# A new order of tasks and banks in the causal attention stage of a two-layer transformer block

## The chip, the core and the metric

The program runs on one core of a Trainium2 chip, in one launch. The core has five engines that work at the same time, each through its own list of instructions in order: PE (TensorE, matrix products), DVE (VectorE), ACT (ScalarE), POOL (GpSimd) and SP (SyncE, which here only issues DMAs). They wait for each other by semaphores. PE writes its results to PSUM, which has eight banks of 128 x 512 floats; the other engines read them out. The metric is the device time of one execution in microseconds (us).

## The reference

The input x is 16 sequences of 512 tokens with 128 features. The reference computes

```
x = x + layernorm( causal_attention( layernorm(x) ) )        # 16 heads of 8, 4 key/value groups, rope
x = x + layernorm( two local layers( layernorm(x) ) )        # 8 heads of 64, windows of 64, gated FFN
```

Only the first line matters here. In it q, k and v are projections of the normalised x with a bias; q and k are turned by rope; `scores = q k^T / sqrt(8)` with the later tokens masked out; `softmax` over the keys; the products with v; a last projection `out @ Wo + bo`; then a layernorm and the addition to x. Four query heads share each of the four key/value groups.

## The kernel before

The program has three stages, one after the other: `causal_attention`, `local_layers` and `last_norm`. The change is in the first.

The causal stage works through the 16 sequences in a software pipeline. The work on one sequence is cut into 198 tasks, and the table `ORDER1` lists them once, as `(part, name, argument)`, with the PSUM bank as a fourth entry where PE fills one. `walk` (line 88) goes through the table once in each step, on every engine: part 0 is done for the next sequence, part 1 for the present one, part 2 for the one before. Each engine takes only its own tasks out of the table, so the table sets the order on every engine, and nothing else does. A task that is moved from part 2 to part 1 is done one step earlier. The class `Plan` (line 24) counts from the same table how often each bank has been filled before, and `Banks` (line 116) turns these counts into waits: a PE task waits until the last content of its bank has been read (`to_fill`), a reader waits until the bank is filled (`to_read`).

The banks are `w0` and `w1` (one PSUM bank each, `a_work` in the trace) for all transposes, projections and the value products, and `pa`, `pb`, `pc` (two PSUM banks each) for the scores.

PE's tasks, with the shape of the part of the array that they use (rows x columns; the trace prints it ahead of the operand's size):

- 128x128: `x_turn`, `q_turn`, `k_turn`, `max_turn`, `attn_turn`, `u_turn` (line 615) and `o_turn` (line 700), four transposes each; `project` (626), `out_project` (711).
- 64x128: `scores` (649, with the mask added by line 654), whose only use is the row maximum; `scores_t` (673), the same products turned, for the exponentials. 22 and 24 tasks in a sequence.
- 128x32: `values` (686), 16 tasks in a sequence, one for a head of a group and a block of keys. Four of them (0 to 3, 4 to 7, ...) fill one bank.

The others: DVE does `row_max` (583, frees the bank of `scores`), `add_bias`, `high`, `divide`, `out_bias` (598), and for three layernorms `variance` (551 to 557) and `rstd`. ACT does `exp` (515, frees the bank of `scores_t`), `seed` (491 and 493, a logarithm and an exponential between `variance` and `rstd`) and copies out of the `w` banks, such as `copy_o` (519) and `copy_max` (509). POOL does `select` (472, the causal mask on the exponentials, before `values` may use them), `rope_cos`, `rope_sin`, `rope_add`, `low`, `apply` (431) and `residual`.

Within one head the chain is `scores` - `row_max` - `max_turn` - `copy_max` - `scores_t` - `exp` - `select` - `values` - `copy_o` - `o_turn` - `divide`.

The wait that a PE task makes for its bank is this:

```
which, before = self.at(name, arg, l, b)
if after and self.at(*after, l, b)[0] != which:
    self.until_read(eng, *after, l, b)
wait(eng, self.freed[which], before)
```

Of the kernel before, what the change touches and what calls it, by code (L numbers as in the profile page):

```python
# [165 lines left out]
OWN_STEPS1 = {"variance": 3, "rstd": 3, "divide": 1}  # L166

ORDER1 = [
    (0, "load", 0), (2, "select", 13), (0, "variance", 0), (2, "select", 15), (2, "scores_t", 19, "pc"),
    (2, "select", 14), (2, "exp", 23), (2, "exp", 19), (2, "values", 8, "w1"), (2, "select", 17), (2, "select", 16),  # L170
    (2, "o_turn", 1, "w0"), (2, "scores_t", 21, "pb"), (1, "row_max", 1), (0, "seed", 0), (2, "values", 9),
    (2, "divide", 1), (2, "select", 23), (2, "scores_t", 20, "pa"), (2, "select", 19), (0, "rstd", 0),
    (1, "scores", 13, "pc"), (2, "exp", 21), (2, "exp", 20), (2, "values", 10), (1, "scores", 6, "pb"),
# [5 lines left out]
    (2, "values", 15), (0, "apply", 0), (1, "row_max", 11), (1, "row_max", 16), (1, "scores", 10, "pc"),
    (0, "x_turn", 0, "w0"), (2, "copy_o", 3), (1, "scores_t", 0, "pb"), (0, "copy_x", 0), (2, "o_turn", 3, "w1"),  # L180
    (1, "exp", 0), (1, "scores", 14, "pa"), (1, "row_max", 10), (2, "divide", 3), (1, "scores_t", 3, "pc"),
    (1, "select", 0), (0, "project", 0, "w0"), (0, "project", 1, "w1"), (1, "scores_t", 1, "pb"), (1, "exp", 3),
    (1, "row_max", 14), (0, "add_bias", 0), (1, "exp", 1), (0, "add_bias", 1), (1, "scores", 5, "pa"),
    (1, "scores_t", 4, "pc"), (1, "row_max", 5), (2, "attn_turn", 0, "w1"), (1, "exp", 4), (2, "copy_attn", 0),
    (1, "max_turn", 1, "w0"), (1, "scores_t", 5, "pb"), (1, "exp", 5), (1, "select", 3), (1, "scores", 17, "pc"),
    (1, "copy_max", 1), (1, "scores_t", 2, "pa"), (0, "rope_cos", 0), (1, "select", 1), (1, "exp", 2),
    (1, "scores", 4, "pb"), (0, "rope_sin", 0), (1, "select", 5), (0, "rope_add", 0), (2, "out_project", 0, "w0"),
    (1, "row_max", 17), (1, "row_max", 4), (2, "out_bias", 0), (1, "scores_t", 7, "pa"), (1, "select", 2),
    (1, "scores", 15, "pc"), (1, "scores_t", 9, "pb"), (1, "exp", 7), (2, "load_again", 0), (1, "exp", 9),
    (1, "values", 0, "w1"), (1, "row_max", 15), (1, "scores_t", 6, "pa"), (0, "high", 0), (1, "scores_t", 8, "pc"),  # L190
    (1, "exp", 6), (1, "select", 4), (1, "values", 1), (1, "exp", 8), (1, "max_turn", 2, "w0"),
    (1, "scores", 21, "pa"), (2, "variance", 1), (0, "copy_v", 0), (1, "copy_max", 2), (1, "values", 2),
    (2, "seed", 1), (1, "values", 3), (1, "scores_t", 11, "pc"), (1, "scores_t", 14, "pb"), (1, "copy_o", 0),
    (0, "low", 0), (1, "row_max", 21), (1, "exp", 11), (1, "scores", 19, "pa"), (0, "q_turn", 0, "w1"),
    (0, "k_turn", 0, "w0"), (1, "scores_t", 10, "pc"), (1, "exp", 14), (0, "copy_q", 0), (1, "scores", 20, "pb"),
    (1, "select", 7), (0, "copy_k", 0), (2, "rstd", 1), (0, "q_turn", 1, "w1"), (2, "apply", 1), (1, "select", 6),
    (0, "k_turn", 1, "w0"), (1, "row_max", 19), (1, "scores_t", 15, "pa"), (2, "residual", 0), (1, "exp", 10),
    (1, "select", 8), (0, "copy_q", 1), (1, "scores", 18, "pc"), (2, "store", 0), (1, "row_max", 20),
    (0, "q_turn", 2, "w1"), (0, "copy_k", 1), (1, "exp", 15), (0, "q_turn", 3, "w0"), (1, "select", 9),
    (0, "copy_q", 2), (1, "select", 10), (1, "scores_t", 16, "pb"), (0, "copy_q", 3), (1, "scores_t", 17, "pa"),  # L200
    (1, "values", 4, "w1"), (1, "exp", 17), (1, "row_max", 18), (0, "scores", 8, "pc"), (1, "exp", 16),
    (2, "variance", 2), (1, "select", 11), (1, "scores_t", 12, "pa"), (2, "seed", 2), (1, "max_turn", 3, "w0"),
    (1, "values", 5), (0, "row_max", 8), (1, "copy_max", 3), (0, "scores", 12, "pb"), (1, "exp", 12),
    (1, "scores_t", 13, "pc"), (2, "rstd", 2), (1, "exp", 13), (1, "o_turn", 0, "w0"), (0, "scores", 0, "pa"),
    (0, "row_max", 12), (1, "scores_t", 18, "pb"), (0, "scores", 9, "pc"), (2, "apply", 2), (1, "values", 6),
    (1, "divide", 0), (1, "select", 12), (1, "values", 7), (2, "u_turn", 0, "w0"), (1, "exp", 18), (0, "row_max", 0),
    (1, "copy_o", 1), (0, "row_max", 9), (1, "scores_t", 23, "pb"), (0, "scores", 1, "pa"), (2, "copy_u", 0),
# [1307 lines left out]
```

## Time and profile before

| | |
|---|---|
| three runs, median (lowest to highest) | 2255.34 us (2254.31 to 2257.92) |
| the profiled execution | 2256.49 us, its span 2254.8 us |
| PE busy over the span | 2030.4 us (90%) |
| DVE, ACT, POOL busy | 1822.7 (81%), 1633.3 (72%), 1379.3 us (61%) |
| first and last PE instruction of the causal stage | at 27.5 us and 755.5 us |
| one step of the causal stage, away from its ends | 42.28 us |

The shares of the whole span mix three stages. The causal stage is a third of it, and its steps repeat: the same row of the timeline comes again 42.28 us later. So one step is enough to read. A row of the timeline gives the start, the time from the first instruction's start to the last one's end, the engine, line, operation and tiles, and how many equal instructions it merges. Matmuls overlap, so what a task takes of PE is read from its start to the start of the next task, not from its own length.

### The profile page before, as it was taken

To read this page: it belongs to the slowest core of one execution; us is meant where nothing else is said; L and a number is where in the kernel's file an instruction comes from. 1 tells how busy PE (TensorE), PEld (TensorE's weight loads), DVE (VectorE), ACT (ScalarE), POOL (GpSimd) and SP (SyncE) were. 2 spreads that over 40 slices of the span, in tenths; PEclk is the share of its full clock that TensorE was granted. 3 is DMA by queue.
4 is the path that set the end of the run, shared out by engine and by line. 5 is a ranking of instruction groups with operands and counts; after the bars stand their busy time and mean duration, and the time that the engine had idled before them with its cause. 6 is when DMAs were issued, how large, how long until landed. Compare 5 with 4: busy or idle time off the path is not lost. (4 is left out here: it accounts for less than half of the span.)

```text
span 2254.8 us, 52451 instructions
## 1 busy us (share of the span) xinstructions
PE 2030.4 (90%) x20476; PEld 1343.0 (60%) x20476; DVE 1822.7 (81%) x3455; ACT 1633.3 (72%) x3312; POOL 1379.3 (61%) x2090
## 2 busy tenths in 40 slices
PE   2999999999999369999999999899999999999971
PEld 1555555555554146666667667666766766766641
DVE  2788888888886366898998988896898899899746
ACT  1577677677677256888888888786888888888745
POOL 3588788788786574655655655564565565565403
PEclk8899999999999679999999999999999999999985
DMA  1001001001000021010010010111001001001013
GB/s 36 1 16 30 15 16 30 15 16 30 15 16 20 29 49 32 19 30 23 18 35 19 18 35 19 29 28 40 19 18 35 19 18 35 19 18 35 19 38 112
DMA packets 50547, 59.92 MB, mean 27 GB/s; under 512 B 8144, under 2 KB 43392, under 8 KB 48256
## 3 DMA queue, kind: packets, MB, share of 16 engines
q1 hardware_dynamic: 50304, 56.58, 10.1%
q8 instruction: 165, 2.70, 0.5%
q14 instruction: 78, 0.64, 0.1%
HBM read 17.90 MB, written 8.39 MB: 12 GB/s over the span
## 5 line engine op out<-in xcount | busy, mean ns | idle before, releaser
L981 POOL TENSOR_TENSOR b_part_b<-b_raw,b_tabs 128x256 f32<-128x256 f32 x512 | 432.2, 874 | 297.5 <-ACT b_raw L1040 262.9
L990 POOL TENSOR_TENSOR b_qk<-b_qk,b_part_b 128x1024 f32<-128x1024 f32 x128 | 332.0, 2594 | 270.6 <-DVE b_qk L1140 263.4
L1140 DVE TENSOR_TENSOR b_qk<-b_raw,b_tabs 128x512 f32<-128x512 f32 x256 | 298.2, 1204 | 0.1
L1241 PE MATMUL b_work<-b_w_high,b_h_high 128*128 128x512 f32 x384 | 190.4, 496 | 30.6 <-DVE b_h_low L1130 19.2
L472 POOL TENSOR_SCALAR_AFFINE_SELECT a_probs<-a_probs 128x256 f32<-128x256 f32 x512 | 205.8, 414 | 0.0
L421 POOL TENSOR_TENSOR a_idle<-a_idle 128x1 f32<-128x1 f32 x432 | 84.5, 196 | 178.8 <-ACT a_probs L515 113.9
L686 PE MATMUL a_work<-a_probs,a_v 128*32 128x512 f32 (+3 forms) x2048 | 178.1, 443 | 8.8 <-POOL a_probs L472 8.5
L1315 PEld LDWEIGHTS b_work<-b_v_even,b_pT 128*64 128x64 f32 x2048 | 137.1, 138 | 78.1 <-issue 72.5
L1061 ACT ACTIVATE b_probs<-b_sb,b_neg_max 128x128 f32<-128x128 f32 x512 | 147.9, 383 | 41.3 <-DVE b_neg_max L1162 40.9
L1067 ACT COPY b_pT<-b_work 128x512 f32<-128x512 f32 x256 | 154.3, 603 | 23.0 <-PE b_work L1305 23.0
L1029 ACT ACTIVATE b_sq<-b_work 128x1024 f32<-128x1024 f32 x128 | 131.7, 1029 | 53.3 <-PE b_work L1243 42.7
L1156 DVE TENSOR_TENSOR b_qk<-b_qk,b_rs 128x1024 f32<-128x1024 f32 x128 | 167.3, 1308 | 3.5 <-POOL b_qk L990 2.2
L583 DVE TENSOR_REDUCE a_qpack<-a_pc 128x2 f32<-128x768 f32 (+1 forms) x128 | 139.4, 1089 | 37.8 <-PE a_pc L654 37.3
L1315 PE MATMUL b_work<-b_v_even,b_pT 128*64 128x66 f32 x2048 | 168.2, 228 | 2.0 <-ACT b_pT L1067 0.8
L1315 PE MATMUL b_work<-b_v,b_pT 128*64 128x66 f32 x2048 | 168.3, 228 | 0.0
L1268 PE MATMUL b_work<-ident,b_qk 128*128 128x128 f32 x1024 | 157.2, 284 | 12.3 <-DVE b_qk L1156 9.9
L1134 DVE TENSOR_REDUCE b_ss<-b_sq 128x16 f32<-128x1024 f32 x128 | 155.1, 1212 | 15.6 <-ACT b_sq L1029 14.4
L583 DVE TENSOR_REDUCE a_qpack<-a_pa 128x2 f32<-128x1024 f32 (+3 forms) x128 | 148.0, 1156 | 15.2 <-PE a_pa L654 13.3
L1305 PE MATMUL b_work<-ident,b_probs 128*128 128x128 f32 x1024 | 155.8, 275 | 3.7 <-ACT b_kT L1048 2.0
L1268 PEld LDWEIGHTS b_work<-ident,b_qk 128*128 128x128 f32 x1024 | 123.0, 145 | 58.0 <-issue 26.0
L1305 PEld LDWEIGHTS b_work<-ident,b_probs 128*128 128x128 f32 x1024 | 123.9, 141 | 55.1 <-issue 36.0
L1242 PE MATMUL b_work<-b_w_low,b_h_high 128*128 128x512 f32 x384 | 153.9, 401 | 0.0
(211 smaller groups left out, 5528.7 us busy)
## 6 DMA issues: line engine op xcount, KB each, us to landing
b_v_even<-b_v SPq DMA_DIRECT2D x32, 528.0 KB, 4.4
b_v_even<-b_v SPq DMA_DIRECT2D x32, 396.0 KB, 5.8
a_x_in<-in_L_attn_x SPq DMA_DIRECT2D x16, 256.0 KB, 3.2
a_x_again<-in_L_attn_x SPq DMA_DIRECT2D x16, 256.0 KB, 3.5
x_scratch<-a_x SPq DMA_DIRECT2D x16, 256.0 KB, 2.4
out<-c_y SPq DMA_DIRECT2D x4, 1024.0 KB, 5.5
b_w_raw<-in_L_ffn_wqkv SPq DMA_DIRECT2D x2, 768.0 KB, 4.2
b_tabs<-tab SPq DMA_DIRECT2D x2, 512.0 KB, 4.2
```

The lines of the kernel that those rows point to most:

```text
L472: last = pool.affine_select(out=a, in_=a, compare_op=ALU.is_ge, fill=0.0, base=0, pattern=[[0, 2], [1, P]], channel_multiplier=-1)
L583: dve.tensor_reduce(qpack[:, slot, i, js[0]:js[-1] + 1, two, NEG_MAX].rearrange("p j g -> p g j"), x[:, :, 0:len(js) * w].rearrange("p g ( ...
L686: last = pe.matmul(bank_of[which][groups(g), s * P:T], v[:, slot, s, g, :], probs_of(j, fill + g % 2)[:, g // 2, col:col + T - s * P], sta ...
L981: last = pool.tensor_tensor(part_b[:, x, :].rearrange("p (h d) -> p h d", d=DH)[:, :, lo:lo + DH // 2], raw[:, i % 2, x, :].rearrange("p ( ...
L990: pool.tensor_tensor(qk[:, i], qk[:, i], part_b[:], ALU.add).then_inc(c_made, 1)
L1134: dve.tensor_reduce(ss[:, i * 16:(i + 1) * 16], sq[:].rearrange("p x (h d) -> p (x h) d", d=DH), AX, ALU.add).then_inc(ss_made, 1)
L1140: last = dve.tensor_tensor(qk[:, i, x, :].rearrange("p (h d) -> p h d", d=DH), raw[:, i % 2, x, :].rearrange("p (h d) -> p h d", d=DH), ta ...
L1156: dve.tensor_tensor(a, a, rs[:, i * 16:(i + 1) * 16].rearrange("p (h a) -> p h a", a=1).to_broadcast([P, 16, DH]), ALU.mult).then_inc(scal ...
L1241: pe.matmul(x, h_high[:, t], w_high[:, cols], start=True, stop=False)
L1268: last = pe.transpose(x[:, p * P:(p + 1) * P], qk[:, i, which, p * P:(p + 1) * P], ident[:])
L1305: last = pe.transpose(x[:, i * P:(i + 1) * P], probs[:, h % 4, i, :], ident[:])
L1315: last = pe.matmul(x[half_rows(w), i * VW:(i + 1) * VW], pT[:, h % 4, w * WIN:(w + 1) * WIN], values_, start=True, stop=True)
```

## The change

Only the table `ORDER1` changes, and with it the waits that `Plan` counts from it; they are kept in kind. The same 198 tasks stand in another order, many with another bank. In the old table PE goes through one step in 49 changes of array shape, counted round from the last entry to the first; in the new one in 41. By shape, the runs of tasks of one shape are 15 of 128x128, 12 of 128x32 and 22 of 64x128 before, and 13, 8 and 20 after. 16 tasks move from part 2 to part 1, so that they are done one step earlier (`scores_t` 19, 21 and 22, `exp` 22 and 23, `select` 13 to 17 and 23, `values` 8 and 9, `o_turn` 1, `divide` 1, and the DMA `load_again`), and two, `scores` 6 and `row_max` 1, from part 1 to part 0. Since the table is one line longer, every line number below it is one higher.

```
-    (0, "load", 0), (2, "select", 13), (0, "variance", 0), (2, "select", 15), (2, "scores_t", 19, "pc"),
+    (0, "load", 0), (0, "variance", 0), (2, "select", 18), (2, "exp", 21), (2, "exp", 19), (1, "row_max", 6),
...
-    (2, "select", 21), (2, "divide", 2), (2, "select", 22), (1, "row_max", 7), (2, "values", 13),
-    (1, "scores", 11, "pb"), (1, "scores", 16, "pa"), (1, "max_turn", 0, "w0"), (2, "values", 14), (1, "copy_max", 0),
+    (1, "row_max", 7), (2, "values", 12, "w0"), (2, "values", 13), (2, "values", 14), (2, "values", 15),
+    (1, "scores", 11, "pb"), (2, "copy_o", 3), (1, "max_turn", 0, "w1"), (0, "x_turn", 0, "w0"), (1, "row_max", 13),
```

PE around `values` 12 to 15 of the sequence before, in a step of the old program: two of them (L686), `scores` 11 and 16 (L649 and L654), `max_turn` 0 (L615), then the other two.

```order
L686 MATMUL a_work<-a_probs,a_v 32x512 x4
L686 MATMUL a_work<-a_probs,a_v 32x384 x4
L649 MATMUL a_pb<-a_kT,a_qT 128x384 x2
L654 MATMUL a_pb<-a_mask_half,a_half_of 128x128 x2
L654 MATMUL a_pb<-a_mask_half,a_half_of 128x64 x2
L649 MATMUL a_pa<-a_kT,a_qT 128x512 x2
L654 MATMUL a_pa<-a_mask_half,a_half_of 128x128 x2
L654 MATMUL a_pa<-a_mask_half,a_half_of 128x64 x2
L615 MATMUL a_work<-ident,a_qpack 128x128 x4
L686 MATMUL a_work<-a_probs,a_v 32x256 x4
L686 MATMUL a_work<-a_probs,a_v 32x128 x4
```

The same place in the new program, from `o_turn` 2 on: `scores` 13 into `pc`, `values` 12 to 15, `scores` 11, `max_turn` 0 and `x_turn`.

```order
L701 MATMUL a_work<-ident,a_oT 128x128 x4
L650 MATMUL a_pc<-a_kT,a_qT 128x512 x2
L655 MATMUL a_pc<-a_mask_half,a_half_of 128x128 x2
L655 MATMUL a_pc<-a_mask_half,a_half_of 128x64 x2
L687 MATMUL a_work<-a_probs,a_v 32x512 x4
L687 MATMUL a_work<-a_probs,a_v 32x384 x4
L687 MATMUL a_work<-a_probs,a_v 32x256 x4
L687 MATMUL a_work<-a_probs,a_v 32x128 x4
L650 MATMUL a_pb<-a_kT,a_qT 128x384 x2
L655 MATMUL a_pb<-a_mask_half,a_half_of 128x128 x2
L655 MATMUL a_pb<-a_mask_half,a_half_of 128x64 x2
L616 MATMUL a_work<-ident,a_qpack 128x128 x4
```

The four value tasks of a head, two visits to the 128x32 shape before, are one visit now.

PE later in the step, before: `values` 1 (L686), `max_turn` 2, `scores` 21 into `pa`, `values` 2 and 3, `scores_t` 11 and 14 (L673), `scores` 19 into `pa` again.

```order
L686 MATMUL a_work<-a_probs,a_v 32x384 x4
L615 MATMUL a_work<-ident,a_qpack 128x128 x4
L649 MATMUL a_pa<-a_kT,a_qT 128x512 x2
L654 MATMUL a_pa<-a_mask_half,a_half_of 128x128 x2
L654 MATMUL a_pa<-a_mask_half,a_half_of 128x64 x2
L686 MATMUL a_work<-a_probs,a_v 32x256 x4
L686 MATMUL a_work<-a_probs,a_v 32x128 x4
L673 MATMUL a_pc<-a_qmT,a_kT 128x256 x2
L673 MATMUL a_pb<-a_qmT,a_kT 128x384 x2
L673 MATMUL a_pb<-a_qmT,a_kT 128x128 x2
L649 MATMUL a_pa<-a_kT,a_qT 128x384 x2
```

The same stretch after: `scores_t` 7 and 6 (the latter into `pb`), `max_turn` 2, `values` 1 to 3, `scores` 20 into `pa`, `scores_t` 11, `q_turn` 0 and `k_turn` 1, and `scores` 21 into `pb`.

```order
L674 MATMUL a_pc<-a_qmT,a_kT 128x512 x2
L674 MATMUL a_pb<-a_qmT,a_kT 128x512 x2
L616 MATMUL a_work<-ident,a_qpack 128x128 x4
L687 MATMUL a_work<-a_probs,a_v 32x384 x4
L687 MATMUL a_work<-a_probs,a_v 32x256 x4
L687 MATMUL a_work<-a_probs,a_v 32x128 x4
L650 MATMUL a_pa<-a_kT,a_qT 128x512 x2
L655 MATMUL a_pa<-a_mask_half,a_half_of 128x128 x2
L655 MATMUL a_pa<-a_mask_half,a_half_of 128x64 x2
L674 MATMUL a_pc<-a_qmT,a_kT 128x256 x2
L616 MATMUL a_work<-ident,a_qpack 128x128 x4
L616 MATMUL a_work<-ident,a_kpack 128x128 x4
```

`max_turn` 2 now stands between `values` 0 and `values` 1, and the second fill of one bank close behind another, `scores` 21 and 19 in `pa`, is gone; instead `scores` 21 fills `pb` behind `scores_t` 6.

ACT in the same stretch of the new program: `exp` 9, 8 and 7, `copy_max` 2 (L510), `seed` 1 (L492 and L494), `copy_o` 0 (L520), `exp` 6 out of `pb`, and the first copies of q and k.

```order
L516 ACTIVATE a_probs<-a_pc 128x1024
L516 ACTIVATE a_probs<-a_pa 128x1024
L516 ACTIVATE a_probs<-a_pc 128x1024
L510 CAST a_qmT<-a_work 128x512
L492 ACTIVATE a_seed<-a_var 128x4
L494 ACTIVATE a_seed<-a_seed 128x4
L520 COPY a_oT<-a_work 128x512
L516 ACTIVATE a_probs<-a_pb 128x1024
L506 CAST a_qT<-a_work 128x512
L502 CAST a_kT<-a_work 128x512
```

Before, all of head 1's first exponentials (`exp` 6 to 9) stood ahead of `seed` 1; now `exp` 6 stands behind it, and with it the bank `pb`.

## Rows read from the trace of the kernel before

**Rows 1.** Stretches: us, busy us (instructions) PE, PEld, DVE, ACT, POOL, clock, DMA.

```profile
318.65:360.93 42.28, 40.96 (x433) 24.72 (x429) 36.41 (x78) 30.71 (x49) 34.65 (x84) 1.00 0.08 21
706.00:758.00 52.00, 28.15 (x253) 14.13 (x251) 17.15 (x72) 23.24 (x38) 29.50 (x74) 0.78 0.06 16
```

**Rows 2.** PE's waits in that step: waited for, us in total, times, longest.

```profile
PE a_pa L649 <- DVE a_qpack L583: 0.7, 1, 0.7
PE a_work L686 <- POOL a_probs L472: 0.4, 1, 0.4
```

**Rows 3.** PE's timeline: start, us, engine, line, operation, tiles, count, idle before.

```profile
318.65 0.66 PE L615 MATMUL a_work<-ident,a_xn 128*128 128x128 f32 x4
319.23 0.50 PE L673 MATMUL a_pb<-a_qmT,a_kT 64*128 64x512 f32 x2
319.66 0.66 PE L700 MATMUL a_work<-ident,a_oT 128*128 128x128 f32 x4
...
322.53 0.50 PE L673 MATMUL a_pb<-a_qmT,a_kT 64*128 64x512 f32 x2
322.87 0.39 PE L649 MATMUL a_pa<-a_kT,a_qT 64*128 64x256 f32 x4
...
323.25 0.36 PE L673 MATMUL a_pc<-a_qmT,a_kT 64*128 64x256 f32 x2
...
338.44 1.09 PE L615 MATMUL a_work<-ident,a_qpack 128*128 128x128 f32 x8
339.46 0.39 PE L673 MATMUL a_pb<-a_qmT,a_kT 64*128 64x256 f32 x2
...
345.39 0.48 PE L673 MATMUL a_pb<-a_qmT,a_kT 64*128 64x512 f32 x2
345.70 0.40 PE L649 MATMUL a_pc<-a_kT,a_qT 64*128 64x512 f32 x2
...
348.94 1.07 PE L686 MATMUL a_work<-a_probs,a_v 128*32 128x512 f32 x8
349.94 0.66 PE L700 MATMUL a_work<-ident,a_oT 128*128 128x128 f32 x4
...
350.96 0.85 PE L686 MATMUL a_work<-a_probs,a_v 128*32 128x384 f32 x8
351.74 0.50 PE L673 MATMUL a_pa<-a_qmT,a_kT 64*128 64x384 f32 x4
...
353.96 0.50 PE L649 MATMUL a_pa<-a_kT,a_qT 64*128 64x256 f32 x4
354.30 0.34 PE L654 MATMUL a_pa<-a_mask_half,a_half_of 64*128 64x256 bf16 x4
354.45 0.36 PE L673 MATMUL a_pc<-a_qmT,a_kT 64*128 64x256 f32 x2
354.89 0.50 PE L649 MATMUL a_pb<-a_kT,a_qT 64*128 64x256 f32 x4
355.23 0.34 PE L654 MATMUL a_pb<-a_mask_half,a_half_of 64*128 64x256 bf16 x4
...
356.56 1.71 PE L686 MATMUL a_work<-a_probs,a_v 128*32 128x512 f32 x16
358.20 0.44 PE L649 MATMUL a_pb<-a_kT,a_qT 64*128 64x384 f32 x2
...
360.93 0.66 PE L615 MATMUL a_work<-ident,a_xn 128*128 128x128 f32 x4
```

**Rows 4.** DVE's timeline in the same step: `high`, and a `row_max` of 1024 columns.

```profile
329.49 0.75 DVE L571 CAST a_qpack<-a_turned 128x512 fp32r<-128x512 f32 x1 [0.35 <-POOL a_turned L447]
...
333.24 1.23 DVE L583 TENSOR_REDUCE a_qpack<-a_pa 128x2 f32<-128x1024 f32 x1
```

**Rows 5.** ACT's timeline behind it: the end of `seed` 1, and an `exp`.

```profile
333.47 0.20 ACT L493 ACTIVATE a_seed<-a_seed 128x4 f32<-128x4 f32 x1
...
334.54 1.03 ACT L515 ACTIVATE a_probs<-a_pb 128x1024 f32<-128x1024 f32 x1
```

More of the change, by code:

```diff
@@ L168 @@
 ORDER1 = [
-    (0, "load", 0), (2, "select", 13), (0, "variance", 0), (2, "select", 15), (2, "scores_t", 19, "pc"),
[L170 to L173, printed above, removed]
@@ L174 @@
-    (2, "values", 11), (1, "row_max", 13), (1, "scores", 3, "pa"), (1, "row_max", 6), (2, "select", 18),
-    (1, "row_max", 3), (2, "scores_t", 22, "pc"), (2, "copy_o", 2), (1, "scores", 2, "pb"), (2, "exp", 22),
-    (1, "row_max", 2), (2, "select", 20), (2, "o_turn", 2, "w0"), (1, "scores", 7, "pc"), (2, "values", 12, "w1"),
-    (2, "select", 21), (2, "divide", 2), (2, "select", 22), (1, "row_max", 7), (2, "values", 13),
-    (1, "scores", 11, "pb"), (1, "scores", 16, "pa"), (1, "max_turn", 0, "w0"), (2, "values", 14), (1, "copy_max", 0),
@@ L179 @@
[L179 to L207, printed above, removed]
+    (0, "load", 0), (0, "variance", 0), (2, "select", 18), (2, "exp", 21), (2, "exp", 19), (1, "row_max", 6),
@@ new lines @@
+    (0, "seed", 0), (2, "select", 21), (2, "scores_t", 20, "pb"), (2, "values", 10), (2, "values", 11),
+    (1, "scores", 2, "pc"), (2, "exp", 20), (1, "scores", 3, "pa"), (0, "rstd", 0), (2, "copy_o", 2),
+    (2, "select", 19), (1, "scores", 7, "pb"), (2, "o_turn", 2, "w1"), (2, "select", 20), (1, "row_max", 2),
+    (2, "select", 22), (2, "divide", 2), (1, "scores", 13, "pc"), (0, "apply", 0), (1, "row_max", 3),
+    (1, "row_max", 7), (2, "values", 12, "w0"), (2, "values", 13), (2, "values", 14), (2, "values", 15),
@@ new lines @@
+    (1, "scores", 11, "pb"), (2, "copy_o", 3), (1, "max_turn", 0, "w1"), (0, "x_turn", 0, "w0"), (1, "row_max", 13),
+    (1, "row_max", 11), (1, "scores", 16, "pa"), (1, "copy_max", 0), (1, "scores_t", 0, "pc"),
+    (1, "scores_t", 3, "pb"), (0, "copy_x", 0), (1, "row_max", 16), (0, "project", 0, "w1"), (1, "scores", 10, "pa"),
+    (0, "add_bias", 0), (1, "exp", 0), (1, "scores_t", 1, "pc"), (1, "exp", 3), (1, "row_max", 10),
+    (0, "project", 1, "w0"), (2, "o_turn", 3, "w1"), (1, "select", 0), (1, "scores_t", 4, "pa"), (0, "add_bias", 1),
@@ new lines @@
+    (2, "divide", 3), (1, "scores", 14, "pb"), (1, "exp", 1), (1, "exp", 4), (1, "row_max", 14),
+    (1, "scores", 5, "pc"), (1, "select", 3), (1, "select", 1), (0, "rope_cos", 0), (1, "row_max", 5),
+    (2, "attn_turn", 0, "w1"), (2, "copy_attn", 0), (1, "scores_t", 5, "pa"), (1, "exp", 5), (1, "scores", 4, "pb"),
+    (1, "max_turn", 1, "w0"), (1, "scores", 17, "pc"), (1, "scores_t", 2, "pa"), (1, "copy_max", 1),
+    (2, "out_project", 0, "w1"), (0, "rope_sin", 0), (1, "row_max", 4), (1, "row_max", 17), (1, "exp", 2),
@@ new lines @@
+    (1, "scores", 15, "pb"), (2, "out_bias", 0), (0, "copy_v", 0), (1, "select", 4), (1, "scores_t", 9, "pc"),
+    (1, "scores_t", 8, "pa"), (0, "rope_add", 0), (1, "exp", 9), (1, "row_max", 15), (1, "values", 0, "w1"),
+    (1, "scores_t", 7, "pc"), (1, "select", 5), (1, "scores_t", 6, "pb"), (1, "max_turn", 2, "w0"), (1, "exp", 8),
+    (1, "exp", 7), (0, "high", 0), (1, "select", 2), (1, "copy_max", 2), (1, "values", 1), (2, "variance", 1),
+    (1, "values", 2), (2, "seed", 1), (1, "values", 3), (1, "copy_o", 0), (1, "scores", 20, "pa"), (2, "rstd", 1),
@@ new lines @@
+    (1, "scores_t", 11, "pc"), (1, "row_max", 20), (0, "low", 0), (0, "q_turn", 0, "w0"), (0, "k_turn", 1, "w1"),
+    (1, "exp", 6), (1, "scores", 21, "pb"), (0, "copy_q", 0), (2, "apply", 1), (1, "scores_t", 10, "pa"),
+    (0, "copy_k", 1), (1, "exp", 11), (0, "q_turn", 2, "w0"), (0, "k_turn", 0, "w1"), (1, "scores", 18, "pc"),
+    (1, "row_max", 21), (1, "scores_t", 14, "pb"), (1, "exp", 10), (1, "select", 6), (0, "copy_q", 2),
+    (0, "copy_k", 0), (1, "scores", 19, "pa"), (1, "row_max", 18), (2, "residual", 0), (0, "q_turn", 1, "w0"),
@@ new lines @@
+    (0, "q_turn", 3, "w1"), (1, "select", 11), (1, "exp", 14), (1, "scores_t", 15, "pb"), (0, "copy_q", 1),
+    (1, "row_max", 19), (0, "copy_q", 3), (1, "select", 7), (1, "o_turn", 0, "w0"), (1, "max_turn", 3, "w1"),
+    (1, "select", 8), (1, "scores_t", 16, "pc"), (2, "variance", 2), (1, "select", 10), (1, "exp", 15),
+    (1, "copy_max", 3), (0, "scores", 12, "pa"), (1, "exp", 16), (1, "select", 9), (1, "scores_t", 17, "pb"),
+    (1, "exp", 17), (1, "values", 4, "w1"), (1, "scores_t", 18, "pc"), (2, "seed", 2), (1, "load_again", 0),
@@ new lines @@
+    (2, "store", 0), (1, "exp", 18), (1, "scores_t", 13, "pb"), (0, "row_max", 12), (0, "scores", 9, "pa"),
+    (1, "values", 5), (2, "rstd", 2), (0, "row_max", 9), (1, "values", 6), (1, "exp", 13), (0, "scores", 8, "pc"),
+    (1, "scores_t", 12, "pa"), (1, "exp", 12), (1, "divide", 0), (0, "scores", 0, "pb"), (0, "row_max", 8),
+    (1, "select", 17), (1, "values", 7), (2, "apply", 2), (0, "scores", 1, "pc"), (1, "scores_t", 23, "pa"),
+    (2, "u_turn", 0, "w0"), (1, "copy_o", 1), (0, "row_max", 0), (0, "row_max", 1), (1, "o_turn", 1, "w1"),
@@ L208 @@
+    (1, "select", 15), (1, "exp", 23), (1, "scores_t", 21, "pb"), (1, "scores_t", 22, "pa"), (1, "select", 12),
+    (1, "divide", 1), (1, "select", 13), (1, "select", 14), (1, "select", 16), (1, "scores_t", 19, "pc"),
+    (1, "values", 8, "w1"), (1, "values", 9), (1, "select", 23), (2, "copy_u", 0), (1, "exp", 22),
+    (0, "scores", 6, "pa"),
 ]
```

## The prediction

> **What bounds the kernel now.** I read the shares of the page first, then the stretches, then PE's waits, then PE's timeline. The page only says that PE is busiest, over three stages that have nothing to do with each other. The stretch of one step of the causal stage says more: from one `x_turn` to the next are 42.28 us, and PE is busy for 40.96 of them, DVE for 36.41, POOL for 34.65 and ACT for 30.71, at the full granted clock [rows 1, 3]. So PE sets the step, with 1.32 us idle. The waits name where most of that is: 0.7 us before a `scores` for the bank `pa`, which DVE's `row_max` frees late, and 0.4 us before a `values` for POOL's `select` [rows 2]. That leaves two things that a new order can change: what PE's own work takes, and these waits. PE's work is the same list of matmuls. But the same task does not take the same time everywhere.
>
> **What a change of array shape costs.** The time of a task is read from its start to the next one's [rows 3].
> - Four transposes alone between tasks of the 64x128 shape: 319.23 - 318.65 = 0.58. Eight in one run: 339.46 - 338.44 = 1.02. Two runs made one save 2 x 0.58 - 1.02 = 0.14.
> - `values` of 512 columns alone: 349.94 - 348.94 = 1.00; of 384 columns: 351.74 - 350.96 = 0.78; the two in one run: 358.20 - 356.56 = 1.64. Again 0.14 for a run less.
> - `scores_t` of 512 columns inside a run: 345.70 - 345.39 = 0.31; first in a run: 322.87 - 322.53 = 0.34; alone: 319.66 - 319.23 = 0.43. So entering costs 0.03 and leaving 0.09.
> - `scores` of 2 x 256 columns inside a run: 323.25 - 322.87 = 0.38; first in a run: 354.45 - 353.96 = 0.49. Entering costs 0.11.
> - The same `scores` behind a wait inside a run (it starts at 354.89) takes as long to its mask as the one that enters: 0.34 in both. A wait inside a run costs the entrance once more, 0.11.
>
> **The change, part by part.** 128x128 has 2 runs less: -0.28 us in a step. 128x32 has 4 less, `values` 12 to 15 in one visit among them: -0.56. 64x128 has 2 less, but what its runs begin with changes: 10 of 22 began with `scores`, 13 of 20 do now. Before: 22 x 0.09 + 10 x 0.11 + 12 x 0.03 = 3.44; after: 20 x 0.09 + 13 x 0.11 + 7 x 0.03 = 3.44. Nothing. If leaving costs 0.05 or 0.13 instead, this comes to -0.2 or +0.1. PE's work: -0.84 us in a step (-1.0 to -0.7).
>
> The waits. The 0.7 us went to `scores` 19, which refilled `pa` close behind `scores` 21. In the new order `pa` goes from `scores` 20 to `scores_t` 10, and to `scores` 19 only five PE tasks after that: gone. The 0.4 us went to `values` 1. Now `max_turn` 2 stands ahead of it, 0.58 of work that covers it; POOL has one `select` and the copy of v more to do before the `select` in question, so between 0 and 0.7 may be left. I take 0, since the move on PE alone is larger than the wait.
>
> New waits, both at places where a bank is refilled:
> - `scores` 13 takes `pc` from `scores` 2, so it waits for `row_max` 2. PE has `scores` 2 (0.49), `scores` 3 and 7 (about 0.38 each, one leaving) and `o_turn` 2 (0.58) in between, 1.8 in all. `scores` 2 lands about 0.68 after its start (from 353.96 to the end of the mask at 354.30 + 0.34), and a `row_max` takes 1.2 [rows 3, 4]: 1.9, and 0.1 for two semaphores. So at least 0.2; ahead of `row_max` 2 stand `row_max` 6 and the three steps of `rstd` 0, and I take 0.4.
> - `scores` 21 takes `pb` from `scores_t` 6, and so waits for `exp` 6, which stands on ACT behind `copy_o` 0 and `seed` 1; and `seed` 1 waits for DVE's `high` and `variance` 1. From the start of `high` to the end of `seed` 1 the trace of before has 329.49 to 333.67, 4.2 us without a gap [rows 4, 5]. `high` can start about 1.6 after `scores` 15 does (`out_bias` and `row_max` 15 are ahead). Then `copy_o` 0 (about 0.5) and `exp` 6 (1.03): 7.3. PE's work from `scores` 15 to `scores` 21 is about 6.6, estimated by kind from rows 3: two `scores` 0.8, five `scores_t` 1.8, four `values` 2.4, three sets of transposes 1.6. Some 0.6 is left as idle time, in `scores` 21 itself or in the `q_turn` ahead of it, which waits for POOL's `low` behind the same `high`.
> - Small ones, `scores_t` 10 behind `row_max` 20 among them: 0.2, as before (1.32 less 0.7 and 0.4).
>
> New sum of waits 1.2, against 1.3: -0.1. All of them stand where the shape changes anyway, while three of the old ones (`scores` 19, 2 and 4) stood inside a run and cost the entrance again, 3 x 0.11: -0.3. Bounds: all waits gone, -1.6; `values` 1 kept at 0.7 and `scores` 13 at twice its size, +0.7.
>
> A step: -0.84 - 0.1 - 0.3 = -1.24, 42.28 to about 41.0. With 16 sequences there are 14 steps in which all three parts run: -17.4. The first and last steps: PE is idle for nearly half of the end [rows 1], so saved work counts for little; the moved tasks leave the end emptier, but the chain through the last layernorms stays. I take -1, between -3 and +2. The two later stages are untouched. Together -18.4: the profiled execution's 2256.49 would be 2238.1. The median of the runs is 1.15 below that execution, so 2255.34 - 18.4 = 2236.9, and I say 2237. With the ends above, a step saves between 0.3 (work -1.0 to -0.7, waits up to +0.4 net of the restarts) and 2.0: 2247 to 2227. SP has nothing new to wait for: `load_again` is issued a step earlier, for a buffer that was read in the step before.
>
> One rule speaks on just this. The Trainium skill, page "TensorEngine Tiling (Array Packing)", section "Key Properties", says that changing the tiling mode, not merely the tile, drains TensorE. The trace agrees that it costs (0.14 for a run of transposes). As a drain it would be the same for every change; the trace has 0.03 for entering with `scores_t` and 0.11 with `scores`. What a uniform price would give is the first rival.
>
> **The rivals.**
> - *Every change costs the same.* The whole cost before is 15 x 0.14 + 12 x 0.14 + 3.44 = 7.22 us a step, 0.147 for each of 49. Eight less: -1.18; with waits and restarts -1.58, x 14 and the ends: -23.1, 2232. For it: the entrance of `scores` may be a matter of which weights come next and not of the shape. Against: three pairs of rows that show otherwise. The drain rule would be borne out by this.
> - *The work saved turns into waiting.* DVE is busy for 36.41 of 42.28, and a loop through DVE, ACT and PE (`scores`, `row_max`, `max_turn`, `exp`, `values`) might hold the step where it is: the 1.24 come back at `scores` 13 and 21. Then only the ends move: 2254. For: new waits stand behind DVE and ACT. Against: even at 41.0 DVE has 4.6 us to spare, and the longest old wait on it goes.
> - *Slower.* `seed` 1 holds up ACT, and with it `copy_o` 0, `exp` 6 and the bank `pb`. Each us by which `out_project`, `out_bias` or `high` comes later than I count goes one to one into `scores` 21. From 1.84 us there instead of 0.6 nothing is gained; at 2.8 a step is 1.0 longer, 14 x 1.0 = 14, 2269. For it: `exp` 6 stood ahead of `seed` 1 before. Against: the path was counted with an unbroken row of the trace, and `out_project` and `out_bias` have no new wait that I can find.
> - *The change doesn't do what it says*: the count of 49 and 41 is of the table and certain; nothing here.
>
> **How the numbers follow.** Forecast 0.74, uniform price 0.10, work into waiting 0.09, slower 0.07. Within 0.2% (4.5 us, about what a measurement can tell from no change) lies only the third case. Faster 0.84, same 0.09, slower 0.07. The forecast's own range, 2227 to 2247, holds the first rival too, and leaves out about 0.16; it stays as it is.
>
> **What would show it.** A step of about 41.0 between two `x_turn`; `values` 12 to 15 in about 2.4 with one entrance; no wait of `values` 1 and of `scores` 19; waits of some 0.4 at `scores` 13 behind `row_max` and 0.6 around `q_turn` 0 and `scores` 21 behind ACT; PE's busy time in a step down by about 1 us, to 39.8 or so. I am wrong if PE's busy time falls by less than 0.5, if its waits in a step exceed 2, or if a step still takes 42.

## The result and the profile after

| | before | after |
|---|---|---|
| four runs each, median (lowest to highest) | 2256.6 us (2254.31 to 2257.92) | 2220.18 us (2218.19 to 2221.09) |
| the profiled execution, its span | 2256.49, 2254.8 us | 2221.09, 2219.4 us |
| one step of the causal stage | 42.28 us | 39.73 us |

The ratio is 0.9838, with an interval of 0.9821 to 0.9856. The forecast was faster, 2237, with a range of 2227 to 2247: the sign is right, but the time lies 7 us below the range, and the gain is twice as large, 36 us instead of 18.

Nearly the whole gain lies in the steps. In the trace of before, the third of the 16 `x_turn` stands at 107.19 us and the last at 656.93: 13 steps in 549.74. After, it is 105.99 to 622.98, 516.99: 32.75 less, 2.52 a step. The two steps ahead of these give 1.8, the part behind the last `x_turn` 2.2 (98.6 to 96.4 until PE's last instruction of the stage); the first `x_turn` comes 0.6 later, and the later stages take 0.7 more.

The stretch of one step after, and of the stage's end (to 2.5 us past PE's last instruction, as in [rows 1]): us, then busy us (instructions) of PE, PEld, DVE, ACT, POOL, clock, DMA.

```profile
344.60:384.33 39.73, 39.53 (x431) 25.03 (x430) 35.61 (x79) 30.01 (x48) 34.68 (x84) 1.00 0.08 21
669.90:721.90 52.00, 28.84 (x268) 16.18 (x262) 17.72 (x73) 24.57 (x40) 29.14 (x73) 0.79 0.04 11
```

PE is idle for 0.20 us of a step, against 1.32 in [rows 1], and its busy time is down by 1.43. The view of PE's waits for this stretch, which had two rows before [rows 2], has none. PE's timeline of the places that the prediction spoke of: start, us, engine, line, operation, tiles, count.

```profile
359.11 0.36 PE L674 MATMUL a_pc<-a_qmT,a_kT 64*128 64x256 f32 x2
359.62 0.66 PE L616 MATMUL a_work<-ident,a_qpack 128*128 128x128 f32 x4
360.11 0.60 PE L616 MATMUL a_work<-ident,a_kpack 128*128 128x128 f32 x4
360.64 0.50 PE L650 MATMUL a_pb<-a_kT,a_qT 64*128 64x512 f32 x2
...
378.36 0.50 PE L650 MATMUL a_pc<-a_kT,a_qT 64*128 64x256 f32 x4
378.71 0.34 PE L655 MATMUL a_pc<-a_mask_half,a_half_of 64*128 64x256 bf16 x4
378.86 0.48 PE L650 MATMUL a_pa<-a_kT,a_qT 64*128 64x256 f32 x4
379.18 0.34 PE L655 MATMUL a_pa<-a_mask_half,a_half_of 64*128 64x256 bf16 x4
379.33 0.42 PE L650 MATMUL a_pb<-a_kT,a_qT 64*128 64x384 f32 x2
379.59 0.26 PE L655 MATMUL a_pb<-a_mask_half,a_half_of 64*128 64x128 bf16 x4
379.78 0.66 PE L701 MATMUL a_work<-ident,a_oT 128*128 128x128 f32 x4
380.44 0.49 PE L650 MATMUL a_pc<-a_kT,a_qT 64*128 64x512 f32 x2
380.77 0.26 PE L655 MATMUL a_pc<-a_mask_half,a_half_of 64*128 64x128 bf16 x4
380.96 2.36 PE L687 MATMUL a_work<-a_probs,a_v 128*32 128x512 f32 x32
383.25 0.44 PE L650 MATMUL a_pb<-a_kT,a_qT 64*128 64x384 f32 x2
```

`values` 12 to 15 take one visit of 383.25 - 380.96 = 2.29. `scores` 13 starts 0.66 after `o_turn` 2, where a set of transposes takes 0.58 [rows 3]: it waits 0.08, not 0.4. `q_turn` 0 starts 0.51 after a `scores_t` of 256 columns that leaves its run, where this takes 0.29 (323.25 to the next task at 323.54 in the trace of before): 0.22 of waiting. `scores` 21, at 360.64, starts 0.53 after `k_turn` 1, which is what transposes inside a run take before they leave: it does not wait.

What DVE and ACT did there, after: `high` and the last operation of `variance` 1; the end of `seed` 1, `copy_o` 0 and `exp` 6; and `row_max` 2.

```profile
355.51 0.48 DVE L572 CAST a_qpack<-a_turned 128x512 fp32r<-128x512 f32 x1
357.69 0.99 DVE L558 TENSOR_SCALAR a_var<-a_mv 128x4 f32<-128x4 f32 x1
379.16 1.23 DVE L584 TENSOR_REDUCE a_qpack<-a_pc 128x4 f32<-128x1024 f32 x1 [0.29 <-PE a_pc L655]
```

```profile
358.95 0.21 ACT L494 ACTIVATE a_seed<-a_seed 128x4 f32<-128x4 f32 x1
359.06 0.57 ACT L520 COPY a_oT<-a_work 128x512 f32<-128x512 f32 x1
359.52 1.03 ACT L516 ACTIVATE a_probs<-a_pb 128x1024 f32<-128x1024 f32 x1
```

From the start of `high` to the end of `seed` 1 are 359.16 - 355.51 = 3.65, not the 4.2 of [rows 4, 5]. `exp` 6 ends at 360.55, and `scores` 21 follows at 360.64. `row_max` 2 had nothing ahead of it: DVE was idle for 0.29 before.

### Where the gain came from

A wait on PE is larger than the idle time that a row shows, because the end of a matmul in the trace lies behind the point from which the next one could start. Two waits of a step before, beside the same kind of task without one: a `scores_t` of 384 columns inside a run, and the `scores` behind it.

```profile
325.12 0.48 PE L673 MATMUL a_pa<-a_qmT,a_kT 64*128 64x384 f32 x4
325.65 0.50 PE L649 MATMUL a_pb<-a_kT,a_qT 64*128 64x256 f32 x4
...
333.46 0.40 PE L673 MATMUL a_pb<-a_qmT,a_kT 64*128 64x384 f32 x4
334.52 0.44 PE L649 MATMUL a_pa<-a_kT,a_qT 64*128 64x384 f32 x2 [0.65 <-DVE a_qpack L583]
...
337.68 0.50 PE L673 MATMUL a_pa<-a_qmT,a_kT 64*128 64x384 f32 x4
338.02 0.39 PE L649 MATMUL a_pc<-a_kT,a_qT 64*128 64x384 f32 x2
```

Without a wait this takes 0.34 with the entrance, so 0.31 inside a run. `scores` 19 comes 1.06 after: 0.75 of waiting, where its row says 0.65. `scores` 4 comes 0.53 after: 0.22 of waiting, and its row says nothing, since 325.12 + 0.48 reaches to 0.05 before it.

I measured every PE task of a step in this way, against the usual time of its kind and place from start to start.

| us in a step | before | after |
|---|---|---|
| PE's work by kind and place, without waits | 39.99 | 39.19 |
| the rest of the step: waits and restarts | 2.28 | 0.55 |
| of it at places that can be named | 2.2: `scores` 19 0.74, `values` 1 0.43, `scores` 2 0.24, `scores` 4 0.21, `u_turn` 0.14, `o_turn` 2 0.13, `out_project` 0.13, `q_turn` 0 0.10, `max_turn` 0 0.08 | 0.86: `q_turn` 0 0.22, `scores_t` 10 0.22, `attn_turn` 0.11, `scores` 7, `o_turn` 2, `values` 7 and `scores` 13 0.07 to 0.08 each |

Not every entry is a wait. `o_turn` 2, `out_project` and `q_turn` 0 of before (0.36) stand behind `scores` 2, 4 and 19, which had waited themselves: these are the entrances paid again that the prediction had at 0.33. `attn_turn`, `scores` 7 and `o_turn` 2 of after (0.26), and `max_turn` 0 of before (0.08), stand behind a `scores` that itself follows another `scores`, and there the second one takes some 0.09 more without a wait (last section). The three of after can't be waits: the `divide`, `exp` and `copy_o` that they need ended at 349.79, 378.85 and 379.32, and they start at 350.09, 379.33 and 379.78. Without these entries the lists come to 2.1 before, 0.36 of it restarts, and 0.6 after. So the table can be wrong by some 0.2: waits and restarts fell by 1.5 to 1.7, and the work by 0.8 to 1.0. Some two thirds of the gain are waits.

### The profile page after: what moved, and what is told of

It reads as the page before. It is cut to its first block and busy times, and to the rows that moved or that the text cites. A ratio compares the mean times of both kernels' runs of the same rounds, so it can differ in the third digit from the quotient of the medians.

```text
span 2219.4 us, 52419 instructions
## 1 busy us (share of the span) xinstructions
PE 2010.5 (91%) x20476; PEld 1350.0 (61%) x20476; DVE 1806.2 (81%) x3455; ACT 1623.4 (73%) x3312; POOL 1380.4 (62%) x2090
## 5 line engine op out<-in xcount | busy, mean ns | idle before, releaser
L584 DVE TENSOR_REDUCE a_qpack<-a_pa 128x2 f32<-128x1024 f32 (+2 forms) x128 | 143.7, 1122 | 44.0 <-PE a_pa L655 41.4
L687 PE MATMUL a_work<-a_probs,a_v 128*32 128x512 f32 (+3 forms) x2048 | 164.9, 440 | 0.2
L1244 PE MATMUL b_work<-b_w_high,b_h_low 128*128 128x512 f32 x384 | 154.1, 401 | 0.0
```

Source lines behind the costliest of these rows:

```text
L687: last = pe.matmul(bank_of[which][groups(g), s * P:T], v[:, slot, s, g, :], probs_of(j, fill + g % 2)[:, g // 2, col:col + T - s * P], sta ...
```

## The experiments

Each ratio is to runs of before on the same chip. Kernels whose name begins with old have the old order, and those with new the new one.

**old_s19 and old_var: is the longest old wait a gap of its own?** `scores` 19 waits 0.74 us in each of 14 steps. Two ways to remove it alone, in the old order: the task moves two PE places, or the operation of DVE that delays it changes its form.

```
-    (1, "scores", 19, "pa"), (0, "q_turn", 0, "w1"), (0, "k_turn", 0, "w0"),
+    (0, "q_turn", 0, "w1"), (0, "k_turn", 0, "w0"), (1, "scores", 19, "pa"),
```

> The old order with one task moved: `scores` 19, the one that waits 0.7 us for `pa`, stands behind `k_turn` 0 instead of ahead of `q_turn` 0; still 49 changes of shape. If the wait is a local one (the bank comes free late and nothing else hangs on it), it goes, with the repeated entrance: a step of 42.28 - 0.8 = 41.5, some 12 us less in all. If the old step was held by a chain through DVE and ACT that comes round once a step (`out_project`, `variance` 1, `seed` 1, `apply` 1, `residual`, `variance` 2, `apply` 2, `u_turn`), PE only waits elsewhere: at `q_turn` 0 for `w1` and at `u_turn`, about 0.5 each, and the step stays at 42.3 (2255 to 2257 us).

```
-                step(dve.tensor_scalar(var_3[:, k], mv[:, :, 1], EPS, None, ALU.add))
+                step(dve.scalar_tensor_tensor(var_3[:, k], mv[:, :, 1], EPS, mv[:, :, 1], ALU.add, ALU.max))
```

> The old order, unchanged, with the last instruction of `variance` as a scalar_tensor_tensor (x + eps, then the maximum with x: the same value). In the trace of before this instruction, on four numbers, takes 1.31 us in `variance` 1 and ends when POOL's copy in `low` ends (333.20 against 333.17); I expect about 0.25 us of the new form, as for the other scalar_tensor_tensor of that size. If a chain through it holds the old step: 42.28 - 0.9 = 41.4, about 14 us less, with the wait of `scores` 19 nearly gone and 49 changes of shape as ever. If only changes of shape matter: nothing, 2256 us. If the instruction takes as long in the new form (POOL holds DVE up whatever it runs): nothing too, and its row says so.

old_s19: 2257.33 us, ratio 1.0004 (0.9994 to 1.0013), a step of 42.33: nothing. PE's waits in a step of old_s19 (waited for, us in total, times, longest):

```profile
PE a_work L686 <- POOL a_probs L472: 0.5, 1, 0.5
PE a_work L615 <- POOL a_z L431: 0.4, 1, 0.4
PE a_work L615 <- ACT a_oT L519: 0.4, 1, 0.4
```

The row of `scores` 19 [rows 2] is gone, and two new ones stand there: `u_turn` behind `apply` 2 (0.14 before, 0.48 from start to start now), and `q_turn` 0 behind `copy_o` 0 (about 0.4). old_var: 2252.49, ratio 0.9987 (0.9978 to 0.9997), 2.7 us. Its operation took 1.04 instead of 1.31 (0.25 was expected), the wait of `scores` 19 fell from 0.74 to 0.14, and that of `u_turn` rose to 0.49. So this wait is no gap that can be closed by itself: what is saved at one place is waited for at the next, behind POOL or ACT.

**old_u and old_s19_u: are these the two ends of one chain?** If the old step is held from `out_project` through the layernorm's steps to `u_turn`, then `u_turn` moved later, together with `scores` 19, sets it free.

```
-    (2, "u_turn", 0, "w0"), (1, "exp", 18),
...
-    (0, "scores", 1, "pa"), (2, "copy_u", 0),
+    (0, "scores", 1, "pa"), (2, "u_turn", 0, "w0"), (2, "copy_u", 0),
```

> Old order, with `u_turn` moved six table entries later, behind the next PE tasks (50 changes of shape instead of 49). In the old order `u_turn` waits 0.145 us a step for `apply` 2, while `scores` 19 waits 0.74 us. If the old step is held by the chain from `out_project` through the three layernorm steps to `u_turn`, then the place of `scores` 19 still holds it first and this alone gives at most the 0.145, less an entrance of about 0.11: step 42.2 to 42.4, 2254 to 2258. If each wait counted for itself, the same 0.145 would go: not told apart here. It is the control for the next kernel.

> Old order, with both moves: `scores` 19 behind `k_turn` 0, and `u_turn` six entries later. `scores` 19 alone gave nothing (step 42.31), since the wait turned up at `u_turn` (0.145 to 0.48). Chain theory: the two waits are the two ends of one chain, so with both loosened the 0.48 at `u_turn` goes, less one more entrance (0.11): step 41.9 to 42.0, 2250 to 2252, though neither move alone gives anything. Rival (there is a further wait that takes it, `scores_t` 23 or `scores` 2 for `pb`): 42.2 or more, 2255. From the waits that remain (`q_turn` 0 about 0.37, `values` 1 about 0.5) even the chain theory leaves the old order far above the new one.

old_u: 2257.6, ratio 1.0005 (0.9996 to 1.0015), a step of 42.46, above the expected 42.2 to 42.4: the wait of `u_turn` went, but `scores` 1, behind which PE now changes shape, takes 0.17 more, and `values` 1 waits 0.09 longer in most steps. old_s19_u: 2254.56, ratio 0.9996 (0.9986 to 1.0006), 42.17. One step of old_s19_u, as stretch and as PE's waits:

```profile
360.27:402.44 42.17, 41.04 (x433) 24.72 (x429) 36.63 (x78) 30.23 (x49) 34.67 (x84) 1.00 0.07 20
```

```profile
PE a_work L686 <- POOL a_probs L472: 0.5, 1, 0.5
PE a_work L615 <- ACT a_oT L519: 0.4, 1, 0.4
```

The 0.4 at `u_turn` is gone, and a step is 0.16 shorter than in old_s19, where 0.3 to 0.4 was expected. Some 0.15 went to one more change of shape, 0.13 to `scores` 2 and `scores_t` 23, which wait longer for `pb`, and 0.07 to `values` 1. So the chain explains where the wait of `scores` 19 went, but it is not the one thing that holds the old step: `values` 1 behind POOL and `q_turn` 0 behind ACT stay, with 0.9 together. My theory of a single chain falls. What is shown is that two moves on PE don't bring the old order's waits below about 2.0 a step; the new one has 0.55. Which of its other moves does that (of PE's tasks, of banks, or on the other engines) was not taken apart.

**new_split: how much is the shape, how much the waits?** In the new order four `scores` move between tasks of another shape, so that 49 changes stand there again, as before, and the waits stay.

```
-    (2, "values", 10), (2, "values", 11), (1, "scores", 2, "pc"),
+    (2, "values", 10), (1, "scores", 2, "pc"), (2, "values", 11),
...
+    (1, "max_turn", 0, "w1"), (1, "scores", 16, "pa"), (0, "x_turn", 0, "w0"),
...
-    (1, "row_max", 11), (1, "scores", 16, "pa"), (1, "copy_max", 0),
...
+    (1, "values", 5), (0, "scores", 8, "pc"), (2, "rstd", 2),
...
-    (1, "exp", 13), (0, "scores", 8, "pc"), (1, "scores_t", 12, "pa"),
...
+    (1, "values", 8, "w1"), (0, "scores", 6, "pa"), (1, "values", 9),
...
-    (1, "exp", 22), (0, "scores", 6, "pa"),
```

> The new order with four tasks moved so that the 41 changes of shape are 49 again: `scores` 8 between `values` 5 and 6, `scores` 6 between `values` 8 and 9, `scores` 2 between `values` 10 and 11, `scores` 16 between `max_turn` 0 and `x_turn`. By the rows: 4 runs more of 128x32 or 128x128 at 0.14, 4 more of 64x128 at 0.09 for leaving, entrances 3 x 0.03 + 0.11: 1.1 us a step, 40.8, about 16 us over the changed kernel, 2236. By a uniform price of 0.147: 1.2, 2237. If the gain was in the waits alone: 39.7 and 2220. If the new order had only moved waits about: new ones here, and more than 2240.

2236.57 us, ratio 0.9912 (0.9896 to 0.9929). The stretch of one step, and two places of it:

```profile
352.71:393.52 40.81, 40.60 (x433) 24.84 (x429) 35.58 (x79) 30.27 (x49) 34.73 (x84) 1.00 0.08 21
```

```profile
383.35 1.06 PE L686 MATMUL a_work<-a_probs,a_v 128*32 128x512 f32 x8
384.35 0.44 PE L649 MATMUL a_pa<-a_kT,a_qT 64*128 64x384 f32 x2
384.63 0.26 PE L654 MATMUL a_pa<-a_mask_half,a_half_of 64*128 64x128 bf16 x4
384.82 0.85 PE L686 MATMUL a_work<-a_probs,a_v 128*32 128x384 f32 x8
385.60 0.50 PE L673 MATMUL a_pb<-a_qmT,a_kT 64*128 64x384 f32 x4
```

Two `values` in two visits take (384.35 - 383.35) + (385.60 - 384.82) = 1.78, against 1.64 in one [rows 3]: the 0.14 of the prediction once more. The waits are those of after (`q_turn` 0 and `scores_t` 10 0.22 each). So these eight changes cost 40.81 - 39.73 = 1.08 a step, 0.135 each, and some 16 us in all; the prices by kind gave 40.8, a price of 0.147 for each 40.9, too close to set them apart. And with as many changes as before, the new order is still 18.6 us faster (2255.15 for before on that chip). The eight are not the same eight: by the prices of the prediction new_split has 0.28 more work in a step than before (one run less of 128x32 and of 128x128, two more of 64x128, four more that begin with `scores`). Its step is still 1.47 shorter, so by this estimate some 1.75 are waits and restarts.

**new_late: the rival on the slower side.** `exp` 6 moves behind `copy_q` 0 on ACT.

```
-    (1, "exp", 6), (1, "scores", 21, "pb"), (0, "copy_q", 0),
+    (1, "scores", 21, "pb"), (0, "copy_q", 0), (1, "exp", 6),
```

> The new order with `exp` 6 one place later on ACT, behind `copy_q` 0, which itself waits for `q_turn` 0. This is the mechanism of the slower rival, put in by hand: `exp` 6 then ends at about 17.35 us of the step instead of 16.07, and `scores` 21, which PE reaches at 16.16, starts 1.2 later. If each us goes one to one into the step: 40.95, some 17 us more, 2237. If PE catches it up at later waits: under 40.3, 2228.

2237.09, ratio 0.9922 (0.9906 to 0.9939). PE's waits in a step, the stretch, and ACT's row of `exp` 6:

```profile
PE a_pb L649 <- ACT a_probs L515: 1.2, 1, 1.2
```

```profile
352.59:393.32 40.73, 39.43 (x430) 24.99 (x429) 34.84 (x79) 30.21 (x48) 34.66 (x84) 1.00 0.08 21
```

```profile
368.89 1.03 ACT L515 ACTIVATE a_probs<-a_pb 128x1024 f32<-128x1024 f32 x1
```

A wait of 1.24 at `scores` 21 made the step 1.0 longer (the 0.2 of `scores_t` 10 went into it). So a late `exp` 6 does go into the step nearly one to one, and the new order stands 0.1 us from it (360.55 to 360.64).

**new_hit, new_low, new_var, new_low_var: what delays `seed` 1?** In new_hit, `select` 2 stands behind `rope_add`, so that POOL does it beside `high`, as I thought it did before.

```
+    (0, "rope_add", 0), (1, "select", 2),
...
-    (0, "high", 0), (1, "select", 2),
```

> The new order with one task moved on POOL: `select` 2 directly behind `rope_add`, ahead of `select` 5, so that its two long operations run beside DVE's `high`. In the profile of before they did, and `high`'s first cast took 0.75 us; in the changed kernel it took 0.48 beside shorter ones, 0.43 alone. If that is why my wait at `scores` 21 did not come: `high` 0.75 again, `seed` 1 and `exp` 6 some 0.3 later, 0.2 to 0.3 of waiting at `q_turn` 0 or `scores` 21, a step of 39.95, 2223 to 2224. If the length of `high` is not on the path: 39.73 and 2220.

2220.24, ratio 0.9846 (0.983 to 0.9862): no change. `high` stayed at 0.47; one of POOL's `select` took 0.59 instead of 0.40. My reason for the 0.75 of [rows 4] is not borne out. (Nor is 0.75 the rule: in 3 of 14 steps of before `high` took 0.43.) The steps are of two kinds, though: in 4 of the 13 between the third and the last `x_turn` the last operation of `variance` 1 took 0.58, and these take 39.54; in the others it took 1.08, and seven of those nine take 39.78. The other operation on this path, the last of `variance` 1, writes 128x4 and takes 0.17 at its shortest (after, the least of 48). In new_low POOL's largest copy goes last; new_var is the edit of old_var in the new order.

```
-                pool.tensor_copy(heads(slot, 16), heads(slot, 0))
...
-                last.then_inc(packed, 1)
+                pool.tensor_copy(heads(slot, 16), heads(slot, 0)).then_inc(packed, 1)
```

> The new order; in POOL's `low` the copy of 512 columns (line 460) stands last instead of third. The last instruction of `variance` 1, on four numbers, ended 0.03 us behind that copy in both profiles (0.99 and 1.31 us long). If that copy alone holds it: it ends behind the next copy instead, of 64 columns, and takes about 0.6; `seed` 1 and `exp` 6 come 0.35 earlier, and a step is 0.1 to 0.2 shorter, 2217 to 2219. If anything on POOL holds it until `low` is over: 1.9 us, `exp` 6 some 0.9 later, 0.8 more in a step, 2231. If POOL has nothing to do with it: 0.99 and 2220.

> The new order with the same instruction in `variance`. PE has only 0.2 us idle in a step of 39.73 there. If waits are all that is left on this path: 0.2 to 0.35 less in a step, 3 to 5 us less than the changed kernel's 2220, so 2215 to 2217. If PE's own work bounds it now: 2220.

> New order with both changes to what stands beside `variance` 1: its last operation as scalar_tensor_tensor, and POOL's 512-column copy in `low` last. Each alone took away the wait of `scores_t` 10 (0.2 us a step) and gave 3.3 us. If both act on the same wait they don't add up: step 39.5, 2216 to 2217. If they add up: 39.3, 2213 to 2214. I expect the first.

new_low: 2216.91, ratio 0.9831 (0.9814 to 0.9847); new_var: 2216.94, 0.9825 (0.9808 to 0.9841); both: 2216.38, 0.982 (0.9803 to 0.9836). The operation took 0.61, 0.35 and 0.34; each alone took away the 0.2 of `scores_t` 10, and together they give no more, as expected. One step of new_low and one of new_low_var:

```profile
343.73:383.28 39.55, 39.39 (x430) 25.04 (x429) 35.41 (x79) 30.21 (x48) 34.69 (x84) 1.00 0.08 22
```

```profile
341.97:381.45 39.48, 39.34 (x431) 25.00 (x429) 35.11 (x79) 30.05 (x48) 34.57 (x84) 1.00 0.08 22
```

new_low_var has the lowest median of the study, though new_low and new_var, 0.5 us above, can't be told from it. Its runs (2215.78 to 2216.78) lie below all of after (2218.19 to 2221.09), 3.8 us by the medians, although the two intervals of the ratios overlap; its steps, 0.22 shorter on average, make 3.0 of it.

**new_best: the rest of the waits.** The two edits of new_low_var, and some ten single moves, three of them.

```
-    (2, "values", 10), (2, "values", 11), (1, "scores", 2, "pc"),
+    (1, "scores", 2, "pc"), (2, "values", 10), (2, "values", 11),
...
-    (1, "values", 3), (1, "copy_o", 0), (1, "scores", 20, "pa"),
+    (1, "values", 3), (1, "scores", 20, "pa"),
...
-    (1, "scores", 21, "pb"), (0, "copy_q", 0),
+    (1, "scores", 21, "pb"), (1, "copy_o", 0), (0, "copy_q", 0),
```

> The same two changes, and eleven single moves in the new order with the 41 changes kept: `scores` 2 two places ahead, `copy_o` 0 behind `exp` 6, `row_max` 3 and 8, `copy_v`, `copy_q` 3, `select` 16, `values` 9, `scores` 10 each by a few places. The work of PE stays as it is (39.2 us a step without waits); what is left to gain is the rest of the waits (0.4 us a step). If `copy_o` 0 behind `exp` 6 lets `scores` 21 and `q_turn` 0 go on without waiting and nothing new waits: step 39.3, 2213. If the bank that `copy_o` 0 frees is then late for `k_turn` 1: 39.6 or more, 2218.

2218.46, ratio 0.9829 (0.9812 to 0.9845), a step of 39.68: 0.2 longer than in new_low_var. `scores` 2 waits 0.18 for `pc` now, `values` 10 behind it comes 0.13 later, and `scores_t` 1 0.1. `q_turn` 0 still waits 0.22, so it was not `copy_o` 0 that held it. The gain didn't come, for another reason than the one I had named.

## Why the prediction was wrong

- **What bounds the step.** Right: PE's work and PE's waits. After, PE is busy for 39.53 of 39.73.
- **PE's work, -0.84.** Right in size: -0.8 by the table, and at most -1.0. The prices from [rows 3] held in new_split, with 40.81 for an expected 40.8. Two flaws: leaving at 0.05 or 0.13 gives +0.08 or -0.08 for 64x128, not -0.2 or +0.1; and a `scores` behind a `scores` pays its entrance too, three times after and once before, some +0.2 that the sum left out. So its closeness is in part luck.
- **The two old waits.** Right: those of `scores` 19 and `values` 1 are gone.
- **"New sum of waits 1.2, against 1.3: -0.1", and -0.3 for restarts.** This step failed: it is -1.5 to -1.7 instead of -0.4, and it explains the missing 18 us (1.1 to 1.3 a step; times 14, 15 to 18 us). It was wrong on both sides.
  - The old side was 2.1 to 2.3 and not 1.65 (1.32 and the restarts). I took the idle time of [rows 1, 2] for the waits: the two large ones were 1.17 instead of 1.1, and "small ones: 0.2, as before" were 0.59, at `scores` 2, `scores` 4 and `u_turn`. The restarts were about right (0.36 for 0.33). The waits need the reading from start to start that I used for the shapes in the same text.
  - The new side was 0.55 to 0.6 instead of 1.2. `scores` 13 got 0.08 instead of 0.4, because `rstd` 0 was over when `row_max` 2 came, and `row_max` 2 started 0.11 after the end of the mask. `q_turn` 0 and `scores` 21 together got 0.22 instead of 0.6, because the path to `seed` 1 was 3.65 and not 4.2: `high` 0.48 for 0.75, and `variance` 1 0.99 for 1.31. I had carried over two durations that depend on what POOL does beside them.
- **Sum and range.** The ends of the range don't follow from their own terms. "All waits gone, -1.6" with -0.84 of work is -2.44 a step, 34 us in 14 steps, and with -1 for the ends 2220; I put 2.0 a step and 2227. At the other end 0.3 a step is 2251, not 2247. That these terms meet the measured time would have been luck: 0.55 of waits are left, and the old ones were larger than 1.6.
- **The ends, -1.** -1.6 (0.6 later, 2.2 shorter): close. Why the end is 2.2 shorter was not tried.
- **The rivals.** A uniform price (2232) would not have been enough either; new_split is too close to both prices to choose between them. "The work turns into waiting" is false for this change. In the old order a wait that is taken away does come back elsewhere (old_s19, old_s19_u); no run took work out of the old order, so whether saved work would come back as waiting there is not shown. The slower rival's mechanism is real, as new_late shows, and 0.1 us away.

## What to carry to other kernels

Measure a wait on TensorE from the start of one task to the start of the next against the same task unhindered, not by the idle time in its row; here that found 2.28 us a step, restarts included, where the idle time was 1.32. When an order is replaced as a whole, count all small waits of the old one again, since single moves in it only pass a wait on, while the new one may not have them at all. Don't carry a duration on DVE over from a trace in which another operation of POOL runs beside it.
